# Graph transformer with two mixtures on one core: fillers on TensorE, smaller steps in the graph heads, and a narrower mixture in another order

## What is computed

```python
x = x + gnn(ln(x), edges, edge_features)        # 3 rounds, then attention of 8 heads of 96
x = x + mixture0(ln(x))                         # 8 experts, 768->1536->768, gelu, top 2 with gates
x = x + gat(ln(x), edges)                       # two graph attention layers, below
x = x + mixture1(ln(x))                         # 4 experts, 768->384->768, gelu, top 1

def gat_layer(x, W, att_src, att_dst, bias, src, dst, heads, out_ch):   # 8 heads of 128, then 1 of 768
    h = (x @ W.T).reshape(n, heads, out_ch)
    e = leaky_relu(a_src[src] + a_dst[dst], 0.2)    # a = (h * att).sum(-1)
    ex = exp(e - segment_max(e, dst)[dst])
    alpha = ex / (segment_sum(ex, dst)[dst] + 1e-16)
    return segment_sum(alpha[:, :, None] * h[src], dst) + bias
```

## Time and profile before

| | |
|---|---|
| median of 3 runs | 1389.2 us (1388.77 to 1390.92) |
| profiled execution | 1389.16 us, of which the span is 1387.6 us |
| mean granted clock of PE over the span | 0.952 |
| busy: PE, DVE, ACT, POOL | 1248.7, 922.2, 579.5, 128.2 us |
| largest PE group | L738, 100.6 us in 288 products of 128x384 |

### The profile page before, as it was taken

One profiled execution on the slowest core, in us unless ns is written; L12 is line 12 of the kernel. 1 busy time (PEld: TensorE's weight loads), 2 busy tenths in 40 slices (PEclk: granted clock), 3 DMA queues, 4 the chain that ended last, 5 costly groups with the idle time before them and its releaser, 6 DMA issues.

```text
span 1387.6 us, 18218 instructions
## 1 busy us (share of the span) xinstructions
PE 1248.7 (90%) x6471; PEld 1064.3 (77%) x6471; DVE 922.2 (66%) x1782; ACT 579.5 (42%) x1012; POOL 128.2 (9%) x123
## 2 busy tenths in 40 slices
PE   5999999999999899998779999999986967878876
PEld 3577569979979796666779999999985757775643
DVE  4478573374374474555749999999997689647313
ACT  2011232342332423335228888988881175221110
POOL 0000200000000000013120000000002057100101
PEclk9999999999999999998789999999997989988799
DMA  9420290500500700040466999999995100020286
GB/s 335 158 91 30 85 325 1 189 28 1 213 4 16 301 4 0 1 158 2 148 225 252 379 400 388 385 392 396 383 350 193 43 28 1 1 80 1 93 297 246
DMA packets 82907, 229.72 MB, mean 166 GB/s; under 512 B 5216, under 2 KB 18592, under 8 KB 82720
## 3 DMA queue, kind: packets, MB, share of 16 engines
q1 hardware_dynamic: 74944, 191.96, 37.5%
q0 software_dynamic: 7904, 36.97, 7.2%
HBM read 202.18 MB, written 26.74 MB: 165 GB/s over the span
## 4 chain that ended last, share of the span: by engine, by line
PE 74%; DVE 16%; DMA 4%; issue 3%; ACT 2%; SPq 0%; POOL 0%; ACTq 0%; DVEq 0%; POOLq 0%
PE dve_ps L738 11%; PE dve_ps L740 11%; PE dve_ps L739 11%; PE act_ps L738 4%; PE act_ps L739 4%; PE act_ps L740 4%; PE dve_ps L781 4%; PE dve_ps L827 3%; DMA slot<-in_e1w 2%; PE dve_ps L971 2%; PE act_ps L954 2%; PE act_ps L778 2%; PE act_ps L827 1%; PE dve_ps L1213 1%; DVE part_slot L2119 1%
## 5 line engine op out<-in xcount | busy, mean ns | idle before, releaser
L2110 DVE TENSOR_TENSOR part_slot<-slot,item_hi 128x768 fp32r<-128x768 f32 x150 | 133.0, 946 | 0.3
L1551 ACT ACTIVATE item_hi<-slot 128x768 fp32r<-128x768 f32 x156 | 118.0, 833 | 25.5 <-DMA slot<-in_e0w 20.3
L2119 DVE TENSOR_TENSOR part_slot<-slot,item_hi 128x768 fp32r<-128x768 f32 x132 | 116.5, 950 | 0.8 <-ACT item_hi L1559 0.2
L1559 ACT ACTIVATE item_hi<-slot 128x768 fp32r<-128x768 f32 x132 | 99.2, 832 | 12.4 <-DMA slot<-in_e0w 12.4
L738 PE MATMUL dve_ps<-item_hi,x_hi 128*128 128x384 f32 x288 | 100.6, 349 | 3.6 <-DVE part_slot L2110 2.3
L738 PE MATMUL act_ps<-item_hi,hid_hi 128*128 128x384 f32 x288 | 99.6, 346 | 4.0 <-DVE hid_lo L2311 4.0
L740 PE MATMUL dve_ps<-item_hi,x_lo 128*128 128x384 f32 x288 | 98.4, 342 | 0.0
L739 PE MATMUL act_ps<-part_slot,hid_hi 128*128 128x384 f32 x288 | 98.3, 341 | 0.0
L740 PE MATMUL act_ps<-item_hi,hid_lo 128*128 128x384 f32 x288 | 97.5, 339 | 0.0
L739 PE MATMUL dve_ps<-part_slot,x_hi 128*128 128x384 f32 x288 | 97.1, 337 | 0.0
L1442 ACT ACTIVATE h_t<-act_ps,par 128x256 f32<-128x256 f32 x36 | 21.1, 586 | 121.5 <-PE act_ps L845 121.5
(11 more groups left out here) (403 smaller groups left out, 3218.2 us busy)
## 6 DMA issues: line engine op xcount, KB each, us to landing
slot<-in_e0w SPq DMA_DIRECT2D x48, 2304.0 KB, 10.3
slot<-in_w SPq DMA_DIRECT2D x9, 2304.0 KB, 9.7
slot<-in_e1w SPq DMA_DIRECT2D x12, 1152.0 KB, 6.3
ea_raw<-in_edge SPq DMA_DIRECT2D x8, 1024.0 KB, 5.4
slot<-in_wqkv SPq DMA_DIRECT2D x3, 2304.0 KB, 14.7
xs<-zrow POOLq DMA_DIRECT2D x2, 3072.0 KB, 15.7
ys<-item_y POOLq DMA_DIRECT2D x16, 384.0 KB, 7.0
slot<-in_gw SPq DMA_DIRECT2D x4, 1536.0 KB, 8.7
```

Of the source, the lines that this page charges most:

```text
L1551: go(item_hi[j][k][:, :], slot[s][:, k * D:(k + 1) * D], ACT.Copy).then_inc(up_high[j], 1)
L1559: go(item_hi[j][k][:, :], slot[s][:, k * D:(k + 1) * D], ACT.Copy).then_inc(down_high[j], 1)
L2110: vv.tensor_tensor(part_slot[s][:, ks], slot[s][:, ks], item_hi[j][k][:, :].bitcast(F32), ALU.subtract).then_inc(up_low[j], 1)
L2119: vv.tensor_tensor(part_slot[s][:, ks], slot[s][:, ks], item_hi[j][k][:, :].bitcast(F32), ALU.subtract).then_inc(down_low[j], 1)
```

## The change

Three edits are joined.

- **Second mixture.** `run_items` becomes `narrow_items`. The up and down matrices are loaded in two halves of 128x3x384, each with semaphores of its own, and each half is loaded anew as soon as PE has used it. PE's loop becomes: turn hidden rows of k, up of k+1, turn rows of k+2, down of k. The item rows are loaded one item earlier.
- **Fillers.** `spend(bank, n)` issues n products of a 128x128 matrix of ones with itself into a bank that is free; nobody reads the result. 288 such products stand in PE's program ahead of waits.
- **Graph heads.** The three small steps of 128x4 become eight instructions of 128x1 with scalar operands from memory; two of them stand between the custom instructions. ACT's Exp table is loaded earlier, its eight roundings follow one after each head, and POOL's low parts move to heads 2 to 7.

```diff
+        up_home = [place(f"up_home{j}", [P, 3, HALF], F32, 2 * 4608 + 3 * HALF * j) for j in range(2)]
+        down_home = [place(f"down_home{j}", [P, 3, HALF], F32, 3 * HALF * j) for j in range(2)]
...
+            def up_part(run, expert, j):
+                w = run.up[bass.ds(expert, 1), j * HALF:(j + 1) * HALF, :].rearrange("a k n -> (a k) n")
+                sp.dma_start(up_home[j][:, :, :], kview(w)).then_inc(up_home_in[j], 16)
+
+            def down_part(run, expert, j, home, arrived):
+                w = run.down[bass.ds(expert, 1), :, j * HALF:(j + 1) * HALF].rearrange("a k n -> (a k) n")
+                sp.dma_start(home[j][:, :, :], kview(w)).then_inc(arrived[j], 16)
...
-                with sp.Fori(1, last) as k:
-                    a, v = run.act_after(k - 1), run.dve_after(k - 1)
-                    sp.wait_ge(run.to_act, a + 1)
-                    sp.wait_ge(run.to_dve, v + 1)
-                    load_x(k + 1)
-                    next_up = expert(k + 1)
-                    sp.wait_ge(run.to_dve, v + 1 + run.n_up)
-                    up_of(run, next_up, 0)
-
-                    sp.wait_ge(run.to_dve, run.dve_after(k))
-                    sp.sem_inc(stood, 1)
-                    down_of(run, expert(k), 0, run.down_slots[0])
...
+                with sp.Fori(1, last) as i:
+                    next_up = expert(i + 1)
+                    for j in range(2):
+                        sp.wait_ge(up_done, 2 * i + j + 1)
+                        up_part(run, next_up, j)
+                    sp.wait_ge(row_turned, 2 * (i + 2))
+                    load_x(i + 2)
+                    next_down = expert(i)
+                    for j in range(2):
+                        sp.wait_ge(down_done, 2 * (i - 1) + j + 1)
+                        down_part(run, next_down, j, down_home, down_home_in)
...
+            def spend(bank, n):
+                for _ in range(n):
+                    mm(bank[:, 0:P], ones[:, :], ones[:, :], start=True, stop=True)
...
+            spend(dve_ps[0], 26)
...
+                if i >= NH - 2:
+                    spend(act_bank(HEAD_UNIT[f"turn_a{i}"], a0), (10, 16)[i - NH + 2])
...
+                    spend(act_ps[2 * t % RING], ((0, 12), (9, 7))[run.layer][t - 2])
...
+                spend(act_ps[3], (14, 6)[run.layer])
...
+                    spend(act_ps[3], 5)
...
+                    if isinstance(i, int) and 0 in js:
+                        spend(*((act_ps[3], 5), (up_banks[0][0], 9))[i])
...
+            spend(act_ps[0], 36)
+            pe.wait_ge(rows_taken, 8)
             turn_features(xn2, ACT0["xt2"], DVE0["xt2"], NT * (L + 2))
...
+                spend(act_ps[0], {0: 11, 1: 8, GH - 1: 9, GH: 20}.get(g, 0))
...
+            spend(act_ps[0], 9)
             pe.wait_ge(att_set, 1)
...
+                def turn_row(i):
 
                     if isinstance(i, int) and i < 2:
                         pe.wait_ge(row_kept, 4 * run.layer + 2 * (i + 1))
                     else:
                         pe.wait_ge(run.x_in, 16 * (i - 1))
-                    wait(pe, run.act_freed, a)
-
-                    wait(pe, run.dve_freed, v if isinstance(v, int) else v - 2)
-                    for half, (bank, signal) in enumerate(((act_ps[3], run.to_act), (dve_ps[2], run.to_dve))):
+                    wait(pe, turned_kept, 2 * i)
+                    for half, bank in enumerate(row_banks):
                         for j in range(3):
                             c = 3 * half + j
-                            last = nc.tensor.transpose(bank[:, j * P:(j + 1) * P], item_x[:, c * P:(c + 1) * P], ident[:, :])
-                        last.then_inc(signal, 1)
-
...
+                            turned = nc.tensor.transpose(bank[:, j * P:(j + 1) * P], item_x[:, c * P:(c + 1) * P], ident[:, :])
+                        turned.then_inc(row_turned, 1)
...
+                def turn_wide(i):
+
+                    pe.wait_ge(wide_taken, i + 1)
+                    for j in range(run.blocks):
+                        turned = nc.tensor.transpose(wide_bank[:, j * P:(j + 1) * P], hid[:, j * P:(j + 1) * P], ident[:, :])
+                    turned.then_inc(wide_turned, 1)
+
+                def times_up(i):
+                    pe.wait_ge(turned_kept, 2 * (i + 1))
+                    for k in range(DC):
+                        if k % 3 == 0:
+                            pe.wait_ge(up_home_in[k // 3], 16 * (i + 1))
+                        done = mm(up_bank[:, 0:HALF], item_xt[:, k, :], up_home[k // 3][:, k % 3, :], start=(k == 0), stop=(k == DC - 1))
+                        if k % 3 == 2:
+                            done.then_inc(up_done, 1)
+
+                def times_down(i, home, arrived, loads):
+
+                    wait(pe, y_ready, 2 * i)
+                    pe.wait_ge(wide_bent, i + 1)
                     for half in range(2):
-                        pe.wait_ge(run.dve_freed, v_banks[half])
+                        pe.wait_ge(arrived[half], 16 * loads)
                         for k in range(run.blocks):
-                            last = mm(dve_ps[run.down_banks[half]][:, 0:HALF], hid_t[:, k, :],
-                                      kslot(slots[k // DC], D)[:, k % DC, half * HALF:(half + 1) * HALF],
+                            done = mm(y_banks[half][:, 0:HALF], hid_t[:, k, :], home[half][:, k, :],
                                       start=(k == 0), stop=(k == run.blocks - 1))
-                        last.then_inc(run.to_dve, 1)
-
+                        done.then_inc(down_done, 1)
...
-                    a, v = run.act_after(k), run.dve_after(k)
-                    turn_x(k + 1, a, v)
-                    turn_hidden(v if isinstance(k, int) else v - 2)
-                    times_up(k + 1, a, v)
-
-                    times_down(k, a + 1 + run.n_turn, (v + 2, v + 3) if run.n_up > 1 else (v, v))
+                    turn_wide(k)
+                    times_up(k + 1)
+                    turn_row(k + 2)
+                    times_down(k, down_home, down_home_in, k + 1)
...
+            go(table[:, 0:1], ident[:, 0:1], ACT.Exp)
...
-            go(table[:, 0:1], ident[:, 0:1], ACT.Exp)
-            for k in range(GD // P):
+
+            def high_second_layer(k):
                 ks = slice(k % 4 * D, (k % 4 + 1) * D)
                 go(part_slot[k // 4][:, ks], slot[2 + k // 4][:, ks], ACT.Copy).then_inc(w_high, 1)
...
+                high_second_layer(g)
...
+                a_dst = part_dst[:, 0, :, g % GH]
+
+                def raise_max(t):
+
+                    dve.wait_ge(g_masked, NT * g + t + 1)
+                    return vv.tensor_scalar(gdec[:, b, 1, t:t + 1], gmax[:, b, t:t + 1], a_dst[:, t:t + 1], 0.0, ALU.add, ALU.max)
+
                 for t in range(NT):
-                    vv.tensor_tensor_reduce(out=masked[:, b, t, :], in0=bank[:, :], in1=mask[:, t, :], scale=0.2, scalar=NONE,
+                    vv.tensor_tensor_reduce(out=masked[:, b, t, :], in0=bank[:, :], in1=mask[:, t, :], scale=0.2, scalar=0.2 * FLOOR,
                                             op0=ALU.subtract, op1=ALU.max, accum_out=gmax[:, b, t:t + 1]).then_inc(g_masked, 1)
-                dve.wait_ge(g_masked, NT * (g + 1))
-                a_dst = part_dst[:, 0, :, g % GH]
-                vv.scalar_tensor_tensor(gdec[:, b, 0, :], gmax[:, b, :], 0.2 * FLOOR, a_dst, ALU.max, ALU.add).then_inc(sig.dve_freed, 1)
+                    if t:
+                        then(raise_max(t - 1))
+                raise_max(NT - 1).then_inc(sig.dve_freed, 1)
+                settle()
                 dve.wait_ge(sig.dve_freed, v0 + unit + 1)
-                then(vv.scalar_tensor_tensor(gdec[:, b, 1, :], gdec[:, b, 0, :], 5.0, gdec[:, b, 0, :], ALU.mult, ALU.max))
-                settle()
-                vv.tensor_tensor(gdec[:, b, 2, :], a_dst, gdec[:, b, 1, :], ALU.subtract).then_inc(g_dec, 1)
+                for t in range(NT):
+                    last = vv.tensor_scalar(gdec[:, b, 2, t:t + 1], gdec[:, b, 1, t:t + 1], -4.0, gmax[:, b, t:t + 1], ALU.mult, ALU.subtract)
+                    if t < NT - 1:
+                        then(last)
+                    else:
+                        last.then_inc(g_dec, 1)
...
-                if g < GD // P:
-                    ks = slice(g % 4 * D, (g % 4 + 1) * D)
-                    low_of(2 + g // 4, ks, part_slot[g // 4][:, ks], g)
+                for k in {2: (0,), 3: (1,), 4: (2,), 5: (3,), 6: (4,), 7: (5, 6, 7)}.get(g, ()):
+                    ks = slice(k % 4 * D, (k % 4 + 1) * D)
+                    low_of(2 + k // 4, ks, part_slot[k // 4][:, ks], k)
```

More of the change, by code:

```diff
@@ L683, in _ @@
             sp.wait_ge(sig.to_act, ACT0["gat2"])
-            up_of(run1, 0, 0)
-            down_of(run1, 0, 0, run1.down_slots[0])
-            run_items(run1)
+            for j in range(2):
+                up_part(run1, 0, j)
+            for j in range(2):
+                down_part(run1, 0, j, down_home, down_home_in)
+            narrow_items(run1)
```

(6 more changed lines are left out.)

209 lines of the change are left out of this document (96 added, 113 removed).

## The result

The changed kernel takes 1348.8 us in the median of four runs (1346.3 to 1353.1), the kernel before 1389.0; the ratio of the times is 0.972 (0.969 to 0.975), so it is 2.8% faster. 1343 was forecast, within 1331 to 1366. The span of the profiled execution fell from 1387.6 to 1347.8 us, by 39.8 where 46 were expected.

What follows compares the result with a forecast made beforehand. PE was taken as the bound, busy 1248.7 of 1387.6 us, with idle and half-clock time to win. Fillers 25, graph heads 13 and second mixture 8 sum to 46 us off 1389.2, giving 1343, range 1331 to 1366.

Steps and rivals of the forecast that it cites:

- Fillers, price: Wherever fillers stand: one 128x128 filler product costs 0.243 us, read from spread, about 0.42 at half clock.
- Fillers, value: Attention's end, both mixture entries, second graph layer and smaller places: fillers holding PE's clock up win 25 us in sum.
- the ceiling b·(1-c): Low-clock stretches: with b us of busy PE at clock c, full clock would take b·(1-c) us off PE.
- Each ends just ahead of what PE waits for: PE's gaps of 4.10, 2.27 and 5.32 us: 16, 9 and 20 fillers fit and shift nothing if the clock is up.
- I take 1 off: Last graph head: nine fillers behind the wait for gp_t push its turning back about 2 us; 1 us is deducted.
- the five periods: Graph heads 2 to 6: cheaper small steps cut each 9.09 us period to 7.56, winning 7.7 us in five.
- Start of the heads: First graph heads: roundings' wait goes (2.3 us), small steps of heads 0 and 1 (3.0), POOL's low parts leave (1.0).
- Second mixture: Second mixture's items: halved loads issued earlier and row turning off the path win 8 us.
- the time of an item: Second mixture: an item falls from 10.8 to 9.2 to 9.4 us, set by transfers (390 GB/s) and PE together.
- The clock case: Rival at the fillers: the clock is not held, fillers give 8 to 12 us instead of 25; 1358 us, chance 0.15.
- POOL holding the steps up: Rival in the graph heads: POOL delays the eight small steps, 0.6 us each, a head takes 11.3; 1371 us, chance 0.11.
- Overrun: Rival at the fillers: they outlast their gaps, deciding at 0.42 us each; 1398 us at 0.45, chance 0.04.

## Why the prediction held, and where it was off

- *The sum.* 46 us were forecast, 39.8 came in the profiled execution and 40.2 in the medians.
- *Fillers, price.* 0.243 us forecast from spread; 20 records in 2.40 us (PE, 617.48), 0.24. Right.
- *Fillers, value.* 25 forecast, 16 measured. The step that failed is the ceiling b·(1-c) taken from one execution, as if fillers could remove every low clock that it shows. At attention's end the clock was low for 10.2 us in the trace of before, but 4.1 of the 5.5 us gained there came without any filler. At the entries it seemed to hold, with 7.3 and 4.8 us where 9 and 6 were forecast, but at the second the eight executions with a stage gain of 2.2 to 2.7 leave the fillers some 2 us over the 0.5 without them. There it was luck of the profiled execution that made the term look right.
- *Heads.* The period was right (7.52 against 7.56). "Each ends just ahead of what PE waits for" failed for the fillers of heads 1 and 7, which stand behind the wait; "I take 1 off" was in truth 3.3 by the run without fillers, and 6.9 by the run that puts them ahead of the wait (15.6 against 8.7). Without fillers the heads won 12.0 where the terms give 14 without that deduction: the five periods, from gp_t of head 1 to that of head 6, gave 5.8 of the 7.7, as the first of them did not shrink (9.91 before, 10.01).
- *Start of the heads.* 6.3 forecast (2.3+3.0+1.0). Without fillers gp_t of head 0 gained 4.7 and that of head 1 6.3. The terms inside are partly wrong: the prediction counts 1.53 us for the small steps of head 0, and these met POOL idle before and took 0.16 us each, so nothing was to be won there:

```profile
1118.15 0.16 DVE L2503 SCALAR_TENSOR_TENSOR gdec<-gdec 128x4 f32<-128x4 f32 x1
1118.34 0.16 DVE L2505 TENSOR_TENSOR gdec<-part_dst,gdec 128x4 f32<-128x4 f32 x1
```

- *Second mixture.* 8 forecast, 4.4 to 7.9 measured. The term mis-sized is the time of an item: 9.2 to 9.4 us forecast, 9.7 in the mean of the change's five intervals. Of its parts the rate was 351 instead of 390 GB/s in this execution, and the wait for up_home, which was not to exceed 0.5 us, reached 1.91.
- *Rivals.* The clock case was half right: the clock still fell in or behind the logits of both entries (0.89 and 0.84), which the prediction had named as a sign of being wrong. POOL holding the steps up did not happen, and two runs show which forms it would have happened to. Overrun, with the clock down as the fillers begin, happened at more than the two places of the heads: the 14 fillers ahead of the ranking at the first entry ran mostly at half clock (28 records in 5.00 us) and ended 1.2 us after DVE had set what PE waited for, those at the second entry 1.3 us after.
- *A reading.* The "eight products of the last weigh" are four products in eight records; the difference of 2.3 us stands.

## What to carry to other kernels

A filler belongs ahead of the wait that it bridges, in a bank that is free before that wait; behind it, it was work on the path here. Price a change by stage, by the same instruction in both traces, since an execution can lose several microseconds to a clock fall that has nothing to do with the change. Take the stage from several executions where there are some: what one profile shows for a stage was 5.3 us here and 2.2 to 2.7 in eight others. A small VectorE step beside busy GpSimd was cheap in the form of one column with scalar operands (0.12 us apart), and dear with two inputs or four columns.

## What the runs showed of the hardware

- The same program up to 1093 us had a clock low of 3 us in one execution (678 to 681) and lows of 10 and 3 us in another (677 to 687, 172 to 175), 5.8 us apart at that point.
- Transposes as fillers kept the clock up as products of ones did: 0.89 in 670 to 686 with either.
- Beside GpSimd, four one-column steps took 0.58 us with scalar operands and 2.21 with two inputs; one four-column step with one input took 0.95, and 0.17 with GpSimd idle.
- A clock low lasted 14 us (674 to 688) with TensorE busy 10.00 of 10 us in its second part.
